# State scans of a Mamba layer: nine of sixteen states weighed by their output gate on ScalarE after a turn through TensorE, instead of by VectorE and GpSimd

## The reference, cut to what matters

```python
delta = jax.nn.softplus(dt @ W_dt + b_dt)
A = -jnp.exp(A_log)
dA = jnp.exp(delta[..., None] * A)
dBu = delta[..., None] * Bm[:, :, None, :] * uc[..., None]
def step(h, inp):
    dA_t, dBu_t, C_t = inp
    h = dA_t * h + dBu_t
    y = jnp.einsum('bdn,bn->bd', h, C_t)
    return (h, y)
...
y = ys.transpose(1, 0, 2) + uc * D
y = y * jax.nn.silu(z)
return y @ W_out
```

## Time and profile before

| | us |
|---|---|
| median of 3 runs | 2075.93 (2075.64 to 2077.74) |
| profiled execution | 2079.11 |
| its span | 2077.3 |
| scan stage in it | about 362 to 748 |

### The profile page before, as it was taken

One profiled execution on the slowest core, in us unless ns is written; L12 is line 12 of the kernel. 1 busy time (PEld: TensorE's weight loads), 2 busy tenths in 40 slices (PEclk: granted clock), 3 DMA queues, 4 the chain that ended last, 5 costly groups with the idle time before them and its releaser, 6 DMA issues.

```text
span 2077.3 us, 28232 instructions
## 1 busy us (share of the span) xinstructions
PE 1734.2 (83%) x8084; PEld 1065.3 (51%) x8084; DVE 1591.7 (77%) x2214; ACT 1289.3 (62%) x2925; POOL 1253.6 (60%) x812
## 2 busy tenths in 40 slices
PE   4079886788888883399699998999899899998999
PEld 3057642233333351277634333999744433337999
DVE  5223288999999983033499998899889799998887
ACT  2332187555555532322399997788556799987885
POOL 4735504999999956455199995000389699990000
PEclk9999999999999995699899999999999999999999
DMA  8123382554455512132244544455354244544553
GB/s 286 47 68 111 117 141 84 178 173 174 173 171 180 171 62 66 47 101 88 97 174 164 214 168 147 163 183 183 102 158 115 107 165 173 207 177 140 186 183 102
DMA packets 142908, 298.44 MB, mean 144 GB/s; under 512 B 14464, under 2 KB 85923, under 8 KB 134481
## 3 DMA queue, kind: packets, MB, share of 16 engines
q1 hardware_dynamic: 134610, 280.82, 41.5%
q0 software_dynamic: 8192, 16.30, 2.4%
HBM read 192.38 MB, written 105.25 MB: 143 GB/s over the span
## 4 chain that ended last, share of the span: by engine, by line
PE 38%; DVE 28%; issue 15%; POOL 9%; ACT 6%; DMA 1%; another core or an unknown queue 1%; DVEq 1%; SPq 0%; POOLq 0%; PEldq 0%; ACTq 0%; PEld 0%
PE ps L2224 10%; DVE arena L1605 6%; PE ps L1920 5%; PE ps L1907 5%; DVE arena L1611 5%; DVE arena L1603 5%; PE ps L2198 5%; PE ps L2054 3%; DVE arena L1544 2%; POOL arena L675 2%; POOL arena L650 2%; POOL slot_inputs L601 2%; DVE c_phiT L1544 1%; DVE stats L1273 1%; ACT XT L927 1%
## 5 line engine op out<-in xcount | busy, mean ns | idle before, releaser
L2142 PE MATMUL ps<-arena 128*128 128x512 f32 x512 | 251.9, 615 | 14.3 <-POOL arena L675 14.1
L683 POOL TENSOR_TENSOR arena<-arena 128x864 f32<-128x864 f32 x128 | 210.1, 1642 | 74.9 <-DVE arena L1603 72.1
L2133 PE MATMUL ps<-c_phiT,arena 128*128 128x512 f32 x512 | 243.9, 600 | 5.5 <-DVE arena L1605 5.0
L675 POOL TENSOR_TENSOR arena<-arena 128x1024 f32<-128x1024 f32 x128 | 246.5, 1927 | 0.0
L2224 PE MATMUL ps<-arena 128*128 128x128 f32 x2048 | 240.9, 276 | 0.0
L2224 PEld LDWEIGHTS ps<-arena 128*128 128x128 f32 x2048 | 235.9, 193 | 1.0 <-issue 1.0
L613 POOL DMA_INDIRECT token_outputs<-arena x128 | 124.3, 971 | 152.3 <-DVE arena L1434 114.0
L990 ACT ACTIVATE arena<-arena 128x32 f32<-128x32 f32 x640 | 195.9, 312 | 0.0
L1544 DVE TENSOR_TENSOR_SCAN arena<-ps,arena 128x1024 f32<-128x1024 f32 x84 | 188.0, 2276 | 6.1 <-POOL arena L645 6.1
L704 POOL COPY arena<-arena 128x512 f32<-128x512 f32 x16 | 22.0, 1374 | 279.6 <-PE ps L2186 279.6
L2054 PE MATMUL ps<-arena,c_ident 128*128 128x512 f32 x336 | 161.0, 601 | 26.0 <-POOL arena L650 26.0
(11 more groups left out here) (245 smaller groups left out, 3852.6 us busy)
## 6 DMA issues: line engine op xcount, KB each, us to landing
arena<-input_gates SPq DMA_DIRECT2D x128, 512.0 KB, 3.7
logit_rows<-arena SPq DMA_DIRECT2D x128, 512.0 KB, 2.6
arena<-logit_rows SPq DMA_DIRECT2D x32, 1024.0 KB, 4.9
XN<-logit_rows SPq DMA_DIRECT2D x32, 1024.0 KB, 4.8
arena<-value_rows SPq DMA_DIRECT2D x32, 512.0 KB, 5.0
arena<-slot_inputs SPq DMA_DIRECT2D x32, 258.0 KB
arena<-in_L_ffn_w SPq DMA_DIRECT2D x32, 256.0 KB
arena<-token_outputs SPq DMA_DIRECT2D x16, 512.0 KB, 8.1
```

What stands on the lines that cost most here:

```text
L675: pool.tensor_tensor(Dd[:, r, :].rearrange("p (n q) -> p n q", q=PSLOT), Ed[:, r, :].rearrange("p (n q) -> p n q", q=PSLOT), over(rD[:, r, ...
L683: pool.tensor_tensor(Ed[:, r, PSLOT * NA:].rearrange("p (n q) -> p n q", q=PSLOT), Lc[:, r, PSLOT * NA:].rearrange("p (n q) -> p n q", q=P ...
L2133: ins = pe.matmul(pbank(2 * h + c), xts[:, r // 2, :], phiT[:, at:at + CHUNK], start=True, stop=True)
L2142: ins = pe.matmul(pbank(4 + 2 * h + c), xns[:, r // 2, :], Dd[:, r, CHUNK * c:CHUNK * (c + 1)], start=start, stop=stop, skip_group_check=True)
```

## The change

Nine states of a group (0, 2, 4, 6, 8, 10, 12, 14, 15) are multiplied by C in a turned layout, where C is a value per partition. PE transposes the scanned state in 128x128 blocks, four to a bank, by halves of 512 into banks 0 and 1 (`turn_state`); ACT copies each block to the buffer `turned` (which is `stage`) with the state's C as scale (`weigh_turned`, eight activations of 128 columns a state); PE transposes the blocks back, accumulating in banks 6 and 7 (`add_turned`). POOL multiplies states 1, 3, 5 and 9, DVE states 7, 11 and 13. Further:

- POOL's C rows no longer pass through PSUM and ACT: SP loads them from DRAM, as the B rows, in its own queue between these. C goes to DRAM beside B (`bvals` has 32 rows, `dts` holds rows 0 to 104 of the projection, and `W_dt` moves to rows 96 on).
- The turned C (`CT`, in `W_in`) is made once, by 32 small matmuls of `BCs` and one copy (`output_gates`).
- `skip` and `step_sizes` become ACT copies into the banks, instead of matmuls; `diag_D` goes.
- The orders of all engines are rewritten; `gated` comes after scan n=2 of the next group. A buffer `w` of a turned state is free once it is turned.
- `turned` uses `stage`, so that `ln_apply(2, 0, 0)` waits for the end of all sums.
- Semaphores `LT`, `C` and `mx` are merged into others (`turned`, `weighed`, `mxC`), with their counts shifted.

```diff
-LOW = 96 + RANK + 1 + DS
+LOW = 96 + RANK + 1
...
+TURNED, POOL_STATES, DVE_STATES = (0, 2, 4, 6, 8, 10, 12, 14, 15), (1, 3, 5, 9), (7, 11, 13)
+TURNED_STATES, POOL_TERMS, DVE_TERMS = HALVES * GROUPS * len(TURNED), GROUPS * len(POOL_STATES), GROUPS * len(DVE_STATES)
...
+        CT = W_in[:, :].rearrange("p (a n) -> p a n", n=DS)
+        turned = stage[:, :, :].rearrange("p h (j c) -> p (h j) c", c=P)
...
+        BCf = dts[0:2 * DS, :, :].rearrange("p b t -> p (b t)")
...
+                if n in POOL_STATES:
+                    i = nth(g, POOL_STATES)
+                    if i >= 2:
+                        sp_.wait_ge(sem("term_pool"), i - 1)
+                    else:
+                        sp_.wait_ge(sem("delta"), DT * (CHUNKS - 1 + i))
+                    sp_.dma_start(Cs[:, i % 2, :], bvals[DS + n, TIME * b:TIME * (b + 1)].partition_broadcast(P)).then_inc(sem(f"Cs{i % 2}"), 16)
...
                 if g >= NW:
-                    hold(pool, sem("scan_sum"), g + 1 - NW)
+                    if (g - NW) % DS in TURNED:
+                        hold(pool, sem("turned"), HALVES * (nth(g - NW, TURNED) + 1))
+                    else:
+                        hold(pool, sem("scan_sum"), g + 1 - NW)
...
             for g in range(0, SCANS, 2):
-                if g:
+                if g + 2 < SCANS:
+                    input_term(g + 2)
+                if g and (g - 1) % DS in POOL_STATES:
                     output_term(g - 1)
                 if g + 2 < SCANS:
-                    input_term(g + 2)
                     input_term(g + 3)
-            output_term(SCANS - 1)
             pool.drain().then_inc(sem("stage"), 1)
             experts(1, 2)
...
 
-            def output_gate(g):
-                hold(act, sem("bc"), g)
-                if g // 2 >= 2:
-                    hold(act, sem("term_pool"), g // 2 - 1)
-                else:
-                    act.wait_ge(sem("delta"), DT * (CHUNKS - 1 + g // 2))
-                act.activation(Cs[:, g // 2 % 2, :], pbank(0, 2), ACT.Copy).then_inc(sem("Cs"), 1)
+            def output_gates():
+                act.wait_ge(sem("bc"), 1)
+                act.activation(W_in[:, :], pbank(0), ACT.Copy).then_inc(sem("BCs"), 1)
+
+            def skip(q):
+                b, d = q // DT, q % DT
+                if q:
+                    act.wait_ge(sem("yz"), q)
+                act.activation(pbank(6, 2), uc[:, d, b, :], ACT.Copy, scale=D_skip[:, d:d + 1]).then_inc(sem("scan_fill"), 1)
+
+            def step_sizes(q):
+                b, d = q // DT, q % DT
+                act.wait_ge(sem("weighed"), HALVES * (nth(DS * (q - 1) + 4, TURNED) + 1))
+                act.activation(pbank(0, 2), dlt[d][:, TIME * b:TIME * (b + 1)], ACT.Copy).then_inc(sem("scan_fill"), 1)
+
+            def weigh_turned(g):
+                b, d, n = unit(g)
+                if g == 0:
+                    act.wait_ge(sem("BCs"), CHUNKS + 1)
+                for h in range(HALVES):
+                    act.wait_ge(sem("turned"), HALVES * nth(g, TURNED) + h + 1)
+                    for j in range(4):
+                        ins = act.activation(turned[:, 4 * h + j, :], pbank(h)[:, P * j:P * (j + 1)], ACT.Copy,
+                                             scale=CT[:, PER_BATCH * b + 4 * h + j, n:n + 1])
+                    ins.then_inc(sem("weighed"), 1)
 
             for v in range(CHUNKS - 1):
                 softplus(v)
             decay(0)
             softplus(CHUNKS - 1)
             decay(1)
+            output_gates()
+            act.wait_ge(sem("BCs"), CHUNKS)
+            skip(0)
             for g in range(0, SCANS, 2):
-                output_gate(g + 1)
-                if g + 2 < SCANS:
+                if g + 2 < SCANS and (g < DS or g % DS != 2):
                     decay(g + 2)
+                if g and g % DS == 0:
+                    weigh_turned(g - 1)
                     decay(g + 3)
+                    weigh_turned(g)
+                    decay(g + 4)
+                    skip(g // DS)
+                else:
+                    weigh_turned(g)
+                    if g >= DS and g % DS == 4 and g // DS + 1 < GROUPS:
+                        step_sizes(g // DS + 1)
+                    if g + 3 < SCANS:
+                        decay(g + 3)
+            weigh_turned(SCANS - 1)
...
-                dve.wait_ge(sem("step_ps"), q - 1)
+                dve.wait_ge(sem("scan_fill"), 2 * q - 1)
...
             for g in range(0, SCANS, 2):
                 q = g // DS
                 scan(g)
+                if q and g % DS == 2:
+                    gated(q - 1)
+                if g and (g - 1) % DS in DVE_STATES:
+                    output_term(g - 1)
                 if q and g % DS == 6 and q + 1 < GROUPS:
                     spread_steps_times_u(q + 1)
                 scan(g + 1)
-                output_term(g)
-                if q and g % DS == 0:
-                    gated(q - 1)
 
...
+            dve.wait_ge(sem("scan_sum"), SCANS)
...
+            for j in range(TILES):
+                ins = pe.matmul(pbank(0)[:, DS * j:DS * (j + 1)], BCs[0:96, P * j:P * (j + 1)], row32[:, DS:2 * DS], start=True, stop=True)
+            ins.then_inc(sem("bc"), 1)
+
+            def turn_state(g, h):
+                pe.wait_ge(sem("scan"), g + 1)
+                if g == 0:
+                    pe.wait_ge(sem("BCs"), CHUNKS + 1)
+                elif (g - 1) % DS in DVE_STATES:
+                    pe.wait_ge(sem("term_dve"), nth(g - 1, DVE_STATES) + 1)
+                if g >= DS and g % DS == 6 and g // DS + 1 < GROUPS:
+                    pe.wait_ge(sem("dtu"), g // DS + 2)
+                for j in range(4):
+                    ins = pe.transpose(pbank(h)[:, P * j:P * (j + 1)], w[g % NW][:, CHUNK * h + P * j:CHUNK * h + P * (j + 1)], ident[:, :])
+                ins.then_inc(sem("turned"), 1)
+
+            def add_turned(g, h):
+                if g % DS == 0:
+                    pe.wait_ge(sem("scan_fill"), max(g // DS + 1, 2 * (g // DS)))
+                pe.wait_ge(sem("weighed"), HALVES * nth(g, TURNED) + h + 1)
+                for j in range(4):
+                    ins = pe.matmul(pbank(6 + h)[:, P * j:P * (j + 1)], turned[:, 4 * h + j, :], ident[:, :],
+                                    start=False, stop=False, is_transpose=True, skip_group_check=True)
+                if h == HALVES - 1:
+                    ins.then_inc(sem("scan_sum"), 1)
+
             def spread(g):
                 b, d, n = unit(g)
-                if g % 2:
-                    if g > 1:
-                        pe.wait_ge(sem("term_dve"), g // 2)
-                else:
-                    pe.wait_ge(sem("Cs"), g // 2 + 1)
+                pe.wait_ge(sem("weighed"), HALVES * (nth(g - 1, TURNED) + 1))
                 for h in range(HALVES):
                     ins = pe.matmul(pbank(h), row32[:, DS + n:DS + n + 1].to_broadcast([96, P]),
                                     BCs[0:96, TIME * b + CHUNK * h:TIME * b + CHUNK * (h + 1)], start=True, stop=True)
                 ins.then_inc(sem("bc"), 1)
 
-            def skip(q):
-                b, d = q // DT, q % DT
-                if q:
-                    pe.wait_ge(sem("yz"), q)
-                for h in range(HALVES):
-                    pe.matmul(pbank(6 + h), diag_D[:, d, :], uc[:, d, b, CHUNK * h:CHUNK * (h + 1)], start=True, stop=False)
-
             def add(g):
-                pe.wait_ge(sem("term_pool" if g % 2 else "term_dve"), g // 2 + 1)
+                by_pool = g % DS in POOL_STATES
+                pe.wait_ge(sem("term_pool" if by_pool else "term_dve"), nth(g, POOL_STATES if by_pool else DVE_STATES) + 1)
                 for h in range(HALVES):
                     ins = pe.matmul(pbank(6 + h), ident[:, :], w[g % NW][:, CHUNK * h:CHUNK * (h + 1)],
-                                    start=False, stop=(g % DS == DS - 1))
+                                    start=False, stop=(g % DS == DS - 1), skip_group_check=True)
                 ins.then_inc(sem("scan_sum"), 1)
-
-            def step_sizes(q):
-                b, d = q // DT, q % DT
-                pe.wait_ge(sem("term_dve"), (DS * (q - 1) + 6) // 2)
-                pe.wait_ge(sem("delta"), DT * CHUNKS)
-                for h in range(HALVES):
-                    ins = pe.matmul(pbank(h), ident[:, :], dlt[d][:, TIME * b + CHUNK * h:TIME * b + CHUNK * (h + 1)],
-                                    start=True, stop=True)
-                ins.then_inc(sem("step_ps"), 1)
-                pe.wait_ge(sem("dtu"), q + 1)
 
...
             for g in range(0, SCANS, 2):
-                if g >= DS and g % DS == 6 and g // DS + 1 < GROUPS:
-                    step_sizes(g // DS + 1)
-                spread(g + 1)
-                if g:
-                    if g % DS == 2:
-                        skip(g // DS)
-                    add(g - 2)
-                spread(g)
+                last = g and (g - 1) % DS in TURNED
```

(29 more changed lines are left out.)

40 lines of the change are left out of this document (18 added, 22 removed).

## The result

The changed kernel takes 2067.22 us (median of 7 runs), the kernel before 2077.74 on the same chip: ratio 0.9945, 95% interval 0.9928 to 0.9961. On a second chip the ratio was 0.9956 (0.9942 to 0.997). The forecast was 2071 against 2075.9, a gain of 5; the measured gain is 9 to 10.5, about twice that, and neither interval reaches 1. The profiled execution is 2067.54, its span 2065.4 against 2077.3.

The account below looks back on a forecast made before the run. No engine over 41 us a group; seam waits and half clock make 46.8. 51.0 + 6 x 46.8 + 45.2 = 377.0, plus 2.3, against 385.4: 6.1 less, 1 held back, so 2075.9 - 5 = 2071; range 2052 to 2096.

Parts of the forecast that it names:

- What bounds it, and what each engine gets: Inner group: POOL bound it before; now POOL 39.8, DVE 40.7, PE about 30, ACT 38 us, none over 41.
- The small activation: ACT's 128-column weighing from PSUM with a scale column: 0.27 us each taken, bounds 0.26 to 0.29, upper bound 0.37.
- list of starts: New order of every engine: each start is the later of its last end and the awaited signal plus 0.05 us.
- The seam: Between groups: DVE idles 3.7 us before scan n=5 for its decay, making 44.4 us a group at full clock.
- The clock: PE after a seam's 4.3 us gap: half clock for 3 to 10 us, raising the group to 46.8 us.
- The 1 us held back: Whole kernel: 1 us taken off the 6.1 us gain for signals that the list has at zero.
- Rival (a): Seams: the clock never falls or PE's gap is under 3 us; 22.2 us less, 2054; chance 0.20.
- Rival (d): PE's clock stays at half nearly throughout, by the rule on transposes: 109 us more, 2187; chance 0.05.
- SP's queue: POOL waits 3.7 us for row n=6 behind n=5's gate row; hidden in inner groups, first group takes 51.0.
- Rival (c): DMA: more queueing at 240 GB/s; with 2.0 us of service a group takes 47.4: 2077; chance 0.08.
- Rival (b): ACT's `weigh_turned` ahead of decays: slower small activations, decisive from 0.30 us each; called 2085; chance 0.20.
- The tail: After the last scan: `add_and_measure(2)` starts at 11.6 us instead of 9.3, costing 2.3 us.

Follow-up runs that it names:

- gap filled: Eleven matmuls of 512 columns into unread bank 0 in PE's gap at each seam, added to the changed kernel: 2055.7 us, 0.9892 of the kernel before.
- the zero matmuls: Three matmuls of zeros into the sum's bank in each of PE's two 2 us gaps a group, added to the kernel with state 13 on POOL: 2031.05 us.
- the row was moved: Changed kernel with the C row of n=5 asked for after the input row of n=8: 2064.17 us, 0.996 of the kernel before.
- cut finer: Changed kernel with the first and last of each four small activations cut into two of 64 columns: 2086.78 us, 1.0057 of the kernel before.
- state 13 on POOL: Changed kernel with the seam's skip on TensorE, the C row of n=5 asked for later and state 13's output product moved from DVE to POOL: 2044.44 us.

## Why the prediction was right, and where it was off

**What bounds it, and what each engine gets.** POOL 39.8 forecast, 40.0 measured; DVE 40.7 and 40.7; ACT 38 and 38.1; PE 30 and 33 to 34. With the clock at 1.00 throughout it is 34.1 less 2.6 for the fillers, 31.5; the rest is half clock.

**The small activation** was the largest unknown: 0.27 taken. Eight and the step to the decay take 558.51 - 556.52 = 1.99, pitch 0.249. The record of one is 389 ns long; neighbours overlap. The forecast's list of starts, gone through again with 0.249, is said to give 45.9 a group for 46.8; the list isn't shown, so this is the author's working and no measurement. The Trainium skill ("VectorE: DVE Perf Modes", The TRN2 errata) gives 172 + columns cycles at 1.2 GHz for a PSUM source. Worked out from it, these are estimates of 0.250 for 128, 0.197 for 64 and 0.570 for 512, and the traces agree: 0.249, 0.194 and 0.57 (1.25 for two less a record of 0.68). The section also advises tiles of 512 elements or more, for work with an SBUF source; as a rule of cost that holds here too, the fine cut costs ACT 7.7 us a group. The group pays 1.2 of them, because ACT isn't the bound.

**The seam** was forecast step by step: `skip` at 4.3, weighing of n=2 from 5.8 at full clock. DVE's wait was to be 3.7 at full clock and 1.4 more with the fall; measured 3.4 (gap filled) and 4.65. The group was to be 44.4 without the fall; with the gap filled it is 44.4. That these agree is in part luck: 20 small activations stand in the seam's path, and at 0.249 instead of 0.27 they take 0.4 off it, which waits that the list lacks put back.

**The clock** fell at each seam (twice at the one at 462 us, else once) for 3.4 to 6.8 us in all, within the forecast's 3 to 10, and once more in the middle of the second group. It cost 1.1 a group instead of 2.4. The forecast added it up from 1.4 on the path to n=5 and 1.4, less 0.3, for a late bank of `spread_steps_times_u`. The first is there, 4.5 - 3.4 = 1.1 on average. The second isn't: DVE waits 0.7 us for that bank in six groups.

```profile
L1586 DVE TENSOR_TENSOR XT<-ps,arena 128x1024 f32<-128x1024 f32 x6 | 7.2, 1207 | 0.7 <-ACT ps L952 0.6
```

That "elsewhere in a group the new order leaves PE no gap of over 1.3 us" was wrong: there are two, of 1.97 and of 1.7 to 1.9, and it is these that the zero matmuls had to fill. By the author's list, 46.8 comes down by 0.9 for the small activation and by 0.9 for the clock (45.9 - 43.9 = 2.0 in the list at 0.249, 1.1 measured), and goes up by 0.5 for waits that it lacks (43.9 at full clock where 44.4 is measured), which makes 45.5. The 1 us held back stood for these waits, at too small a size. Rival (a), 2054, is the run with eleven matmuls: 0.9892 of before. Rival (d) is out: the clock was 0.96 over the inner groups shown, and stayed at 1.00 for 362 us with the gap filled, though 144 transposes a group are about half of PE's work. The Trainium skill ("TensorE: Matmul & The Clock Gate", PE-mode transpose) says that a transpose doesn't count as busy for the gate in the way other matmuls do; no run here has transposes alone for long, so these show only that this mix holds the clock.

**SP's queue.** Row n=6 was to come 5.5 after POOL's product of n=1; it came 565.70 - 560.42 = 5.3 after it. POOL's wait was put at 3.7, where 5.5 less one input of 2.0 makes 3.5; measured 3.33. That the seam's wait covers it, and what shows without the cover, was right. Rival (c) did not come: 231 to 237 GB/s at groups of 45, and 263 at 41.8. The first group was to take 51.0, it took 50.1, and 47.2 once the row was moved.

**Rival (b)**: at about 0.32 each (cut finer) the stage was to take 389; it took 391.4, the kernel slower than before by 0.57%.

**The tail**: `add_and_measure(2)` at 11.6 forecast, 746.04 - 734.53 = 11.5 measured. Another 0.7 comes after it in this execution, where a `project_out` runs at half clock behind PE's wait (on the second chip the next chunk comes 4.4 after it, as in the kernel before):

```profile
747.68 3.38 PE L2132 MATMUL ps<-c_W_out,arena 128*128 128x128 f32 x16
```

**The sum.** Forecast 51.0 + 6 x 46.8 + 45.2 = 377.0, measured 50.1 + 6 x 45.5 + 45.1 = 368.4: 8.6 too high, of it 0.9 the first group and 7.7 the groups' two terms; 0.7 too little in the tail. So the mechanism was right and the gain half of the measured one, because the clock's fall and the small activation were priced too high. Measured by the stage, 17.0 less and 3.0 back would be 14 us; the medians show 9 to 10.5. What takes the other 4 us was not found: outside the stage the profiled spans hold 1691.9 us before, 1697.0 and 1695.1 in the two of the changed kernel, and 1688.5 to 1695.5 in its variants. Had the medians shown the whole 14, the forecast would have been further off: the total came nearer than its terms.

## What to carry to other kernels

When work moves so that no engine is full, look for the one point of each round where an instruction last in one queue is first needed by another, and follow the chain from there; add the waits that lie covered beside it, since they are what remains once it is mended. A wait that is mended can lay bare another that gives the gain back, so test a covered wait with its cover removed as well. An engine's time for a run of equal instructions is its pitch times their count, not the record's length times it.

## What had not been expected of the hardware

Work that computes nothing paid for itself twice: eleven matmuls (2.55 us) a seam shortened the stage by 7.3 us, and six records of 0.46 (2.74 us) in each of two gaps of 2 us a group took the kernel with state 13 on POOL from 2044.4 to 2031.1, its stage from 352.4 to 340.3. Four matmuls in the same gap did nothing. An activation of 128 columns with a scale column from PSUM is recorded as 389 ns and comes every 249.
